# Gates, their picking rows and output biases as two rounded float32 parts instead of three bfloat16 ones

## The chip, the cores and the metric

The kernel runs on one core of a Trainium2 chip. The metric is the device time of one execution in microseconds. A run of the kernel before took 4008.13 us in the median of three (4006.91 to 4010.70).

## The reference, cut to what matters

The program is four blocks over x, an array of 2 x 1024 tokens by 128 features. Four of its parts are networks of experts, and they share one procedure in the kernel:

```
b0m: probs = softmax(flat @ Wr + br); only the top expert of 4 kept      (up 128->512, silu, down 512->128, + bias)
b0f: probs = softmax(xn @ router); top 4 of 16 kept, and 2 shared        (128->64, gelu, 64->128, no biases)
b1f: probs = softmax(xn @ gate); each of 8 experts takes its 256 best    (128->512, gelu, 512->128, + bias), and 1 shared
b3f: three trees (q, k, v) choose one of 16 leaves for each token        (128->64, relu, 64->128, + bias)
out[token] = sum over experts e of  gate[token, e] * (act(x @ W1[e] + b1[e]) @ W2[e] + b2[e])
```

Everything is float32 in the reference. The rest (a state space scan, attention of three kinds, six layers of local attention) is not touched by the change.

## The kernel before, in words

Tokens lie along the free dimension: x is a tile of 128 partitions (features) by 2048 columns (tokens), cut into 4 quarters of 512. TensorE takes three kinds of operands here: plain float32, bfloat16, and float32r, a rounded float32. A product of nearly float32 exactness is made from float32r parts: each operand is split into a head (the rounded value) and a tail (the rest), and three products are summed, head by head, tail by head, head by tail.

Each network stage is a chain of short stages with a barrier of all engines between them: `router_probs` (or `walk_trees` in b3f), `keep_top` (or `choose_tokens` in b1f), `to_part_rows` (`to_rows` in b3f), and `mlp`. Within a stage each engine runs its own list in order, and semaphores tie the lists together.

**Gates.** GpSimd first clears the tile `gates` (128 x 2048, bfloat16). `to_part_rows` splits the table of probabilities (tokens by experts) into three bfloat16 parts on VectorE (lines 1208 to 1215: copy, subtract, copy, subtract, copy), TensorE turns the 16 token tiles (line 346), and VectorE copies the turned parts from PSUM into the rows of `gates` (line 361). Before those copies VectorE also splits the output biases into three parts, with the same five instructions for each net. In b3f the gates are zeros and ones, so `to_rows` turns them whole, as plain float32 (line 313), but VectorE still splits three nets' biases before it copies (line 323).

**mlp.** A unit is (group g, quarter i, chunk c). There are 4 groups of 4 chunks in b0m, 9 of 1 in b0f, 9 of 4 in b1f and 24 of 1 in b3f, and with 4 quarters 64, 36, 144 and 96 units. For a unit TensorE issues:

- if the group is gated and c is 0, one bfloat16 product (line 449): a matrix `select` that picks and spreads the expert's gate rows, with `gates`. b0f and b1f have a last group without gates;
- three float32r products for the hidden layer (line 457);
- the output of the unit three places earlier: three float32r products (lines 474, 476, 479), preceded, where a net is opened, by three bfloat16 products of bias and gates (line 469).

ScalarE applies the activation function (line 519), VectorE multiplies by the gate (line 560), ScalarE rounds the product to its head (line 505) and VectorE subtracts for the tail (line 550). ScalarE (line 495) and VectorE (line 532) also split each group's weights, which SyncE's queue fetches (line 434).

Of the kernel before, what the change touches and what calls it, by code (L numbers as in the profile page):

```python
# [16 lines left out]
P = 128  # L17
B, T = 2, 1024
N = B * T
TILES = N // P  # L20
QW = 512
# [187 lines left out]
def router_probs(nc, K, name, flat, weight, bias_row, experts, probs, parts, gates, one_row=None):  # L209


    with ExitStack() as ctx:
# [6 lines left out]
        with stage(nc, "logits_ready", "shifted", "exps_ready", "headed", "tailed", "cleared",  # L219
                   "dve_chain") as (block, S):  # L220

            @block.gpsimd
            def _(pool):
                pool.memset(gates[:], 0.0).then_inc(S.cleared, 1)
                pool.wait_ge(S.cleared, 1)
                if one_row is not None:
                    pool.memset(gates[one_row:one_row + 1], 1.0).then_inc(S.cleared, 1)
                    pool.wait_ge(S.cleared, 2)
                take_tails(pool, flat, parts, S.headed, S.tailed)
# [64 lines left out]
def bias_parts(chain, dve, bias, parts, rest):  # L294

    for n in range(bias.shape[1]):
        split_parts(chain, dve, bias[:, n], [parts[:, n, i] for i in range(3)], rest[:])


def to_rows(nc, K, name, table, rows, short, bias, parts):  # L300


    with ExitStack() as ctx:
        M = Memory(nc, ctx)
        turned = M.ps(f"{name}_turned", [P, QUARTERS, QW])
        bias_rest = M.sb(f"{name}_bias_rest", [P, P])
        per = QW // P
        with stage(nc, "turned_ready", "copied", "dve_chain") as (block, S):
# [9 lines left out]
            @block.vector  # L318
            def _(dve):
                bias_parts(Chain(dve, S.dve_chain), dve, bias, parts, bias_rest)  # L320
                for q in range(QUARTERS):
                    dve.wait_ge(S.turned_ready, q + 1)
                    dve.tensor_copy(short[0:rows, cols(q, QW)], turned[0:rows, q]).then_inc(S.copied, 1)
                dve.wait_ge(S.copied, QUARTERS)

def to_part_rows(nc, K, name, table, rows, short, bias=None, parts=None):


    with ExitStack() as ctx:
        M = Memory(nc, ctx)
        turned = M.ps(f"{name}_turned", [P, QUARTERS, QW])
        split = M.sb(f"{name}_split", [P, TILES, 3, rows], BF16)
        rest = M.sb(f"{name}_rest", [P, TILES, rows])
        bias_rest = None if bias is None else M.sb(f"{name}_bias_rest", [P, P])
        per = QW // P
        wide = 3 * rows
        with stage(nc, "split", "turned_ready", "copied", "dve_chain") as (block, S):  # L340

            @block.tensor
            def _(pe):
                pe.wait_ge(S.split, 1)
                for t in range(TILES):
                    ins = pe.matmul(turned[0:wide, t // per, cols(t % per, P)],
                                    split[:, t].rearrange("p k e -> p (k e)"), K.ident16[:],
                                    start=True, stop=True)
                    if t % per == per - 1:
                        ins.then_inc(S.turned_ready, 1)  # L350

            @block.vector
            def _(dve):
                chain = Chain(dve, S.dve_chain)
                split_parts(chain, dve, table[:], [split[:, :, i] for i in range(3)], rest[:],
                            S.split)
                if bias is not None:
                    bias_parts(chain, dve, bias, parts, bias_rest)
                for q in range(QUARTERS):
                    dve.wait_ge(S.turned_ready, q + 1)  # L360
                    dve.tensor_copy(short[0:wide, cols(q, QW)], turned[0:wide, q]) \
                        .then_inc(S.copied, 1)
                dve.wait_ge(S.copied, QUARTERS)


# [2660 lines left out]
```

## Time and profile before

| | |
|---|---|
| median of three runs | 4008.13 us |
| profiled execution, its own time | 3999.94 us |
| its span, first to last instruction | 3998.2 us |
| TensorE busy | 3499.2 us (88%) |
| VectorE busy | 2983.8 us (75%) |
| ScalarE busy | 2425.5 us (61%) |
| the four mlp stages together | some 530 us of the span |

The span is that of one profiled execution, and 1.7 us of the execution lie around it. A busy matmul row includes the time in which a product drains under the next one, so the spacing of starts, and not the duration, tells what one product costs.

### The profile page before, as it was taken

How to read it: one execution, taken by the hardware profiler on the slowest of the kernel's cores; microseconds unless marked ns; L12 is line 12 of the kernel's file. 1: busy time of each engine (PE TensorE's matmuls, PEld its weight loads, DVE VectorE, ACT ScalarE, POOL GpSimd, SP SyncE). 2: the span in 40 equal slices, each digit the busy share in tenths (PEclk: the TensorE clock that was granted, in tenths of full speed). 3: DMA queues.
4: the chain of work that ended last, by engine and by line, in shares of the span. 5: the costliest groups of instructions: out<-in, count | busy, mean ns of one | idle time of the engine just before them, and what ended most of it. 6: DMA issues, size and time to landing. Idle time of an engine off the chain costs nothing. (4 is left out here: it accounts for less than half of the span.)

```text
span 3998.2 us, 103162 instructions
## 1 busy us (share of the span) xinstructions
PE 3499.2 (88%) x41084; PEld 2106.6 (53%) x41125; DVE 2983.8 (75%) x5780; ACT 2425.5 (61%) x4554; POOL 1393.6 (35%) x634
## 2 busy tenths in 40 slices
PE   7979678888849958999999999999999986998898
PEld 3347433333327735666666666666666663222665
DVE  5958757777739867777778777778778855887685
ACT  3336437777728826676666676676676652555472
POOL 3720011111100007676666675666666630000000
PEclk8979859999969979999999999999999996999899
DMA  1000047777602002322322322322322211100000
GB/s 40 0 6 6 11 161 231 232 232 231 196 12 69 11 0 64 98 61 56 99 60 59 97 59 58 99 57 62 97 58 63 58 42 59 35 25 13 14 15 11
DMA packets 174521, 285.75 MB, mean 71 GB/s; under 512 B 36819, under 2 KB 76628, under 8 KB 172116
## 3 DMA queue, kind: packets, MB, share of 16 engines
q1 hardware_dynamic: 173460, 278.40, 23.8%
q8 instruction: 329, 5.39, 0.6%
q14 instruction: 156, 1.28, 0.1%
q10 hardware_dynamic: 576, 0.69, 0.0%
HBM read 103.97 MB, written 74.45 MB: 45 GB/s over the span
## 5 line engine op out<-in xcount | busy, mean ns | idle before, releaser
L2298 POOL TENSOR_TENSOR b2f_norm<-b2f_norm,b2f_minus_half 128x16 f32<-128x16 f32 x192 | 555.1, 2909 | 275.5 <-DVE b2f_norm L2639 275.5
L2288 POOL TENSOR_TENSOR b2f_q<-b2f_q,b2f_q_part 128x1024 f32<-128x1024 f32 x96 | 228.1, 2376 | 693.7 <-DVE b2f_q_part L2629 693.7
L1720 ACT ACTIVATE b1a_weights<-b1a_b_ps 128x512 f32<-128x512 f32 x512 | 277.2, 596 | 39.4 <-PE b1a_b_ps L1645 37.2
L1835 DVE TENSOR_REDUCE b1a_tops<-b1a_a_ps 128x1 f32<-128x512 f32 (+3 forms) x512 | 244.6, 502 | 19.5 <-PE b1a_a_ps L1601 17.9
L2581 ACT ACTIVATE b2f_v_rows<-b2f_q_ps 128x1024 f32<-128x1024 f32 x96 | 98.3, 1024 | 262.6 <-PE b2f_q_ps L2360 153.5
L1552 POOL TENSOR_SCALAR b1a_k_op<-b1a_k_op,b1a_extra 128x1024 bf16<-128x1024 bf16 x32 | 90.7, 2845 | 446.5 <-DMA b1a_k_op<-part_copies 409.3
L1720 ACT ACTIVATE b3a_weights<-b3a_b_ps 128x512 f32<-128x512 f32 (+3 forms) x384 | 161.2, 502 | 136.8 <-PE b3a_b_ps L1655 135.6
L2638 DVE TENSOR_REDUCE b2f_norm<-xn 128x16 f32<-128x1024 f32 x192 | 234.2, 1220 | 12.0 <-ACT xn L2522 4.8
L2531 ACT ACTIVATE b2f_prob<-b2f_odd_ps,b2f_bias,b2f_norm 128x64 f32<-128x64 f32 x768 | 232.6, 447 | 6.2 <-DVE b2f_bias L2655 4.9
L2531 ACT ACTIVATE b2f_prob<-b2f_even_ps,b2f_bias,b2f_norm 128x64 f32<-128x64 f32 x768 | 232.6, 451 | 2.3 <-DVE b2f_bias L2655 2.3
L2291 POOL TENSOR_TENSOR b2f_k<-b2f_k,b2f_k_part 128x1024 f32<-128x1024 f32 x96 | 227.2, 2367 | 0.7 <-DVE b2f_k_part L2629 0.7
L1728 ACT ACTIVATE b1a_e_sb<-b1a_e_ps 128x512 f32<-128x512 f32 x256 | 153.0, 597 | 121.3 <-PE b1a_e_ps L1587 117.8
L2351 PE MATMUL b2f_q_ps<-b2f_wqkv,b2f_xs 128*128 128x512 f32 x384 | 212.2, 680 | 8.5 <-DVE b2f_kt L2605 5.7
L1830 DVE CUSTOM_DVE_ANT_0 b1a_summed<-b1a_a_ps,b1a_band 128x256 f32<-128x256 f32 (+2 forms) x320 | 142.4, 445 | 95.4 <-PE b1a_a_ps L1601 93.6
L2373 PE MATMUL b2f_q_ps<-b2f_o_cols,b2f_wo 128*128 128x128 f32 x1536 | 192.5, 279 | 4.2 <-ACT b2f_o_cols L2560 2.9
L2360 PE MATMUL b2f_q_ps<-b2f_wqkv,b2f_xs 128*128 128x512 f32 x384 | 190.6, 619 | 0.8 <-ACT xn L2522 0.8
L2351 PE MATMUL b2f_k_ps<-b2f_wqkv,b2f_xs 128*128 128x512 f32 x384 | 185.7, 606 | 0.0
L2373 PEld LDWEIGHTS b2f_q_ps<-b2f_o_cols,b2f_wo 128*128 128x128 f32 x1536 | 180.8, 193 | 6.4 <-ACT b2f_o_cols L2560 3.3
L712 POOL TENSOR_TENSOR b0s_drive<-b0s_raw,xn 128x1024 f32<-128x1024 f32 x32 | 135.1, 4222 | 89.9 <-DVE b0s_raw L728 89.9
L1601 PE MATMUL b1a_a_ps<-b1a_k_op,b1a_q_op 64*128 64x512 bf16 x512 | 139.5, 405 | 23.0 <-DVE b1a_tops L1835 22.5
L2625 DVE TENSOR_TENSOR b2f_q<-b2f_q_ps,b2f_turn 128x1024 f32<-128x1024 f32 x96 | 117.3, 1222 | 48.4 <-PE b2f_q_ps L2351 40.8
L2560 ACT ACTIVATE b2f_o_cols<-b2f_even_ps 128x1024 f32<-128x1024 f32 x48 | 49.2, 1026 | 149.8 <-PE b2f_even_ps L2366 149.7
(528 smaller groups left out, 9301.7 us busy)
## 6 DMA issues: line engine op xcount, KB each, us to landing
b2f_values<-b2f_v_rows SPq DMA_DIRECT2D x1534, 64.0 KB
position_scratch<-b1a_e_sb SPq DMA_DIRECT2D x128, 512.0 KB, 4.0
b1a_band<-position_scratch SPq DMA_DIRECT2D x128, 384.0 KB
b2f_wqkv<-in_b2f_wqkv SPq DMA_DIRECT2D x6, 1536.0 KB, 7.3
b2f_turn<-in_c_rotary SPq DMA_DIRECT2D x6, 1024.0 KB, 8.6
b1f_raw<-in_b1f_both SPq DMA_DIRECT2D x9, 512.0 KB, 3.7
part_copies<-b1a_parts SPq DMA_DIRECT2D x12, 256.0 KB
b2f_wo<-in_b2f_wo SPq DMA_DIRECT2D x6, 512.0 KB, 9.8
```

The costliest lines, as they stand in the source:

```text
L1720: act.activation(weights[:, s % P_RING, c, lo:QW], b_room(s, c)[:, lo:QW], ACT.Exp).then_inc(S.exps_ready, 1)
L1728: act.activation(e_sb[:, a % RING, h], e_ps[:], ACT.Copy).then_inc(S.e_copied, 1)
L1830: ins = dve.tensor_tensor_reduce(summed[:, n % 4, 0:z1 - z0], src, band[:, a % BANDS, h, at0:at0 + z1 - z0], 1.0, LOWEST, ALU.add, ALU.max ...
L1835: ins = dve.tensor_reduce(out, src, AX_X, ALU.max)
L2288: pool.tensor_tensor(G.q[:, g % 2], G.q[:, g % 2], G.q_part[:], ALU.add) \
L2291: pool.tensor_tensor(G.k[:, g % 2], G.k[:, g % 2], G.k_part[:], ALU.add) \
L2298: pool.tensor_tensor(part, part, G.minus_half[:, 0:HEADS], ALU.pow) \
L2351: pe.matmul((Z.q, Z.k)[j // 2][:, j % 2], tile_input(g), G.wqkv[:, l % 2, cols(j, QW)], start=True, stop=True).then_inc(S.qk_ready, 1)
L2360: ins = pe.matmul(Z.q[:, h], tile_input(g), wv[:, :, h], start=True, stop=True)
L2373: ins = pe.matmul(Z.q[:, 0, 0:P], G.wo[:, layer(g) % 2, p], G.o_cols[:, p], start=(p == 0), stop=(p == PAIRS - 1))
L2531: act.activation(G.prob[:, i // 2, i % 2], ps[:, i % 2, cols(i // 2, HD2)], ACT.Exp, bias=G.bias[:, i:i + 1], scale=G.norm[:, g % 3, i:i + ...
L2638: chain(dve.tensor_reduce(norm[:, cols(i, HEADS)], G.squares[:, i], AX_X, ALU.add))
```

## The change

The tile `gates`, the picking matrices and the output biases become float32r. The probabilities are split into two parts, head and tail, not three, and so are the biases; the picking matrices are repeated for two parts. Turned tables are plain float32 transposes in all four stages. The picking matrices arrive in bfloat16 as before, and ScalarE copies them to float32r within `to_rows`. The biases are split on GpSimd, one copy and one subtraction for all nets. The bias product at the opening of a net is two products in place of three.

```diff
-                pool.memset(gates[:], 0.0).then_inc(S.cleared, 1)
+                pool.memset(gates[:].bitcast(F32), 0.0).then_inc(S.cleared, 1)
...
+def to_rows(nc, K, name, table, rows, gates, pick, rounded, bias=None, split=True):
...
+        parts = M.sb(f"{name}_parts", [P, TILES, 2, rows], F32R) if split else None
...
+        wide = 2 * rows if split else rows
...
+                if split:
+                    pe.wait_ge(S.split, 2)
                 for t in range(TILES):
-                    ins = pe.transpose(turned[0:rows, t // per, cols(t % per, P)], table[:, t],
-                                       K.ident[:])
+                    src = parts[:, t].rearrange("p k e -> p (k e)").bitcast(F32) if split else table[:, t]
+                    ins = pe.transpose(turned[0:wide, t // per, cols(t % per, P)], src, K.ident[:])
...
+            @block.scalar
+            def _(act):
+                act.activation(rounded.pick[:], pick, ACT.Copy).then_inc(S.picked, 1)
+                act.wait_ge(S.picked, 1)
+
+            if bias is not None:
+                @block.gpsimd
+                def _(pool):
+                    pool.tensor_copy(rounded.bias[:, :, 0], bias[:]).then_inc(S.bias_headed, 1)
+                    pool.wait_ge(S.bias_headed, 1)
+                    pool.tensor_tensor(rounded.bias[:, :, 1], bias[:], rounded.bias[:, :, 0].bitcast(F32),
+                                       ALU.subtract).then_inc(S.bias_tailed, 1)
+                    pool.wait_ge(S.bias_tailed, 1)
...
-                bias_parts(Chain(dve, S.dve_chain), dve, bias, parts, bias_rest)
+                if split:
+                    dve.tensor_copy(parts[:, :, 0], table[:]).then_inc(S.split, 1)
+                    dve.wait_ge(S.split, 1)
+                    dve.tensor_tensor(parts[:, :, 1], table[:], parts[:, :, 0].bitcast(F32),
+                                      ALU.subtract).then_inc(S.split, 1)
...
-                        for n in range(3):
+                        for n in range(2):
                             pe.matmul(y_ps[:, i], nets[net].bias[:, n], gates[:, tokens(i)],
                                       start=(n == 0), stop=False)
...
-        gates = M.sb("b0f_gates", [P, N], BF16)
+        gates = M.sb("b0f_gates", [P, N], F32R)
```

The last edit is made alike for b0m, b1f and b3f.

## Rows read from the trace of the kernel before

**Rows 1.** The page, busy time of each engine over the span.
```profile
PE 3499.2 (88%) x41084; PEld 2106.6 (53%) x41125; DVE 2983.8 (75%) x5780; ACT 2425.5 (61%) x4554; POOL 1393.6 (35%) x634
```

**Rows 2.** Windows of the four mlp stages: b0m, b0f, b1f, b3f.
```profile
core 0: us, PE busy (x) PEld busy (x) DVE busy (x) ACT busy (x) POOL busy (x), PEclk, DMA share, GB/s
277.00:374.00 97.00, 95.83 (x400) 73.92 (x408) 86.81 (x146) 82.61 (x145) 0.00 (x0) 0.97 0.04 12
433.00:491.50 58.50, 56.98 (x238) 40.86 (x242) 45.57 (x75) 43.60 (x81) 0.00 (x0) 0.96 0.05 14
1198.00:1407.00 209.00, 207.78 (x887) 163.61 (x904) 184.72 (x309) 183.28 (x325) 0.00 (x0) 0.99 0.12 39
3735.00:3900.00 165.00, 163.71 (x689) 112.90 (x702) 134.33 (x222) 122.83 (x215) 0.00 (x0) 0.98 0.06 18
```

**Rows 3.** Waits in b3f's mlp, 3740 to 3895 us, longest first.
```profile
ACT b3f_hidden L519 <- PE b3f_h_ps L457: 36.7, 72, 1.1
DVE b3f_scaled L560 <- ACT b3f_hidden L519: 26.5, 65, 1.0
```

**Rows 4.** Timeline of TensorE, hidden layer's second product: first and last of stretches.
```profile
1230.22 0.40 PE L457 MATMUL b1f_h_ps<-b1f_xn_head,b1f_w_tail 128*128 128x512 f32 x1
...
1378.94 0.40 PE L457 MATMUL b1f_h_ps<-b1f_xn_head,b1f_w_tail 128*128 128x512 f32 x1
...
1384.42 0.39 PE L457 MATMUL b1f_h_ps<-b1f_xn_head,b1f_w_tail 128*128 128x512 f32 x1
...
1404.82 0.39 PE L457 MATMUL b1f_h_ps<-b1f_xn_head,b1f_w_tail 128*128 128x512 f32 x1
...
3754.02 0.39 PE L457 MATMUL b3f_h_ps<-b3f_xn_head,b3f_w_tail 128*128 128x512 f32 x1
...
3795.97 0.39 PE L457 MATMUL b3f_h_ps<-b3f_xn_head,b3f_w_tail 128*128 128x512 f32 x1
...
3805.10 0.39 PE L457 MATMUL b3f_h_ps<-b3f_xn_head,b3f_w_tail 128*128 128x512 f32 x1
```

**Rows 5.** Groups by line and form, TensorE: products and weight loads of b3f.
```profile
L457 PE MATMUL b3f_h_ps<-b3f_xn_head,b3f_w_head 128*128 128x512 f32 x96 | 56.6, 590 | 5.0 <-DVE b3f_w_tail L532 5.0
...
L449 PE MATMUL b3f_g_ps<-b3f_gates,b3f_pick 128*128 128x512 bf16 x85 | 33.7, 397 | 0.0
...
L457 PEld LDWEIGHTS b3f_h_ps<-b3f_xn_head,b3f_w_tail 128*128 128x128 f32 x96 | 18.7, 195 | 2.6
...
L449 PEld LDWEIGHTS b3f_g_ps<-b3f_gates,b3f_pick 128*128 128x128 bf16 x96 | 9.3, 97 | 31.2 <-issue 30.1 <-DVE b3f_scaled L560 1.0
```

**Rows 6.** Timeline of TensorE, plain float32 products of 512 columns, two a row.
```profile
1442.78 1.02 PE L1101 MATMUL b2a_kvr_ps<-xn,b2a_w_now 128*128 128x512 f32 x2
1443.64 1.02 PE L1103 MATMUL b2a_kvr_ps<-xn,b2a_w_ahead 128*128 128x511 f32 x2
```

**Rows 7.** Timeline, b3f's turning of the gates up to the mlp's first instruction.
```profile
3727.52 0.23 DVE L1208 CAST b3f_bias<-b3f_b 128x128 bf16<-128x128 f32 x1 [0.94 <-PEq L42]
3727.53 3.62 PE L313 MATMUL b3f_trees_turned<-c_ident,b3f_reach 128*96 128x128 f32 x16 [5.79 <-PEq L42]
...
3731.84 2.48 DVE L323 CAST b3f_gates<-b3f_trees_turned 96x512 bf16<-96x512 f32 x4
3735.23 0.42 ACT L495 ACTIVATE b3f_w_head<-b3f_raw 128x256 fp32r<-128x256 f32 x1 [30.69 <-PEq L42]
```

**Rows 8.** Timeline, b1f's split and turning of the gates.
```profile
1191.93 0.23 DVE L1208 CAST b1f_split<-b1f_probs 128x128 bf16<-128x128 f32 x1 [0.98 <-PEq L42]
1192.19 0.29 DVE L1209 TENSOR_TENSOR b1f_rest<-b1f_probs,b1f_split 128x128 f32<-128x128 f32 x1
...
1193.39 1.88 PE L346 MATMUL b1f_turned<-c_ident,b1f_split 128*24 128x128 bf16 x16 [3.94 <-DVE b1f_split L1215]
...
1194.68 2.47 DVE L361 CAST b1f_gates<-b1f_turned 24x512 bf16<-24x512 f32 x4
```

**Rows 9.** Groups by line and form, GpSimd and ScalarE: nearest rows for added or widened work.
```profile
L2305 POOL COPY b2f_kt<-b2f_kt 128x256 f32<-128x256 f32 x84 | 53.4, 635 | 0.0
L108 POOL TENSOR_TENSOR b1f_xn_tail<-xn,b1f_xn_head 128x512 fp32r<-128x512 f32 x4 | 5.1, 1294 | 3.4 <-ACT b1f_xn_head L101 3.4
...
L1317 POOL MEMSET b3a_values<- 128x256 f32 x1 | 0.6, 556 | 42.4 <-POOLq L42 42.4
...
L1396 ACT ACTIVATE b3a_parts<-b3a_left 128x1024 bf16<-128x1024 f32 x12 | 12.7, 1057 | 26.8 <-DVE b3a_left L1369 17.6 <-DVE b3a_left L1374 8.3 <-DVE b3a_left L1379 0.6
```

More of the change, by code:

```diff
@@ L291, in _, with rounded_constants @@
                 dve.wait_ge(S.counted, experts + 2)
[L294 to L300, printed above, removed]
+def rounded_constants(I, name, pick, nets):
+    return Names(pick=None if pick is None else I.sb(f"{name}_pick32", list(pick.shape), F32R),
+                 bias=None if nets is None else I.sb(f"{name}_bias", [P, nets, 2, P], F32R))
+def to_rows(nc, K, name, table, rows, gates, pick, rounded, bias=None, split=True):
     with ExitStack() as ctx:
@@ L305, in to_rows @@
         turned = M.ps(f"{name}_turned", [P, QUARTERS, QW])
-        bias_rest = M.sb(f"{name}_bias_rest", [P, P])
+        parts = M.sb(f"{name}_parts", [P, TILES, 2, rows], F32R) if split else None
         per = QW // P
-        with stage(nc, "turned_ready", "copied", "dve_chain") as (block, S):
+        wide = 2 * rows if split else rows
+        with stage(nc, "split", "turned_ready", "copied", "picked", "bias_headed", "bias_tailed") \
+                as (block, S):
             @block.tensor
@@ L322, in _ @@
                     dve.wait_ge(S.turned_ready, q + 1)
[L323 to L362, printed above, removed]
@@ L363, in _ @@
+                    dve.tensor_copy(gates[0:wide, cols(q, QW)], turned[0:wide, q]).then_inc(S.copied, 1)
                 dve.wait_ge(S.copied, QUARTERS)
@@ L604, in block0_ffn @@
             keep_top(nc, "b0f", probs, ROUTED0, TOP0)
-            to_part_rows(nc, K, "b0f", probs, ROUTED0, gates)
-        groups = [Names(net=0, select=K.pick16[:, c], biases=None) for c in range(pairs)]
+            to_rows(nc, K, "b0f", probs, ROUTED0, gates, K.pick16[:], rounded)
+        groups = [Names(net=0, select=rounded.pick[:, c], biases=None) for c in range(pairs)]
         groups.append(Names(net=0, select=None, biases=None))
@@ L821, in block0_attn @@
             rw, rb = weights.router, weights.router_b
-            gates = I.sb("b0m_gates", [P, N], BF16)
-            bias = I.sb("b0m_bias", [P, 1, 3, P], BF16)
+            gates = I.sb("b0m_gates", [P, N], F32R)
+            rounded = rounded_constants(I, "b0m", K.pick4, 1)
             parts = two_parts(I, "b0m_flat", [P, N])
@@ L828, in block0_attn @@
                 keep_top(nc, "b0m", probs, 4, 1)
-                to_part_rows(nc, K, "b0m", probs, 4, gates, b2, bias)
-            groups = [Names(net=0, select=K.pick4[:, e],
+                to_rows(nc, K, "b0m", probs, 4, gates, K.pick4[:], rounded, b2)
+            groups = [Names(net=0, select=rounded.pick[:, e],
                             biases=[b1[:, 4 * e + c:4 * e + c + 1] for c in range(4)]) for e in range(4)]
             mlp(nc, K, "b0m", parts, weights.stock, groups, ACT.Silu,
-                [Names(dst=flat, add=True, bias=bias[:, 0])], gates)
+                [Names(dst=flat, add=True, bias=rounded.bias[:, 0])], gates)
         layer_norm(nc, K, "b0n", flat, x, gain=w.ln_w, offset=w.ln_b, add_to=x)
@@ L1015, in block1_ffn @@
         b2 = later("b1f_b2", [P, 1, P])
-        gates = M.sb("b1f_gates", [P, N], BF16)
-        bias = M.sb("b1f_bias", [P, 1, 3, P], BF16)
+        gates = M.sb("b1f_gates", [P, N], F32R)
+        rounded = rounded_constants(M, "b1f", K.pick8, 1)
         parts = two_parts(M, "b1f_xn", [P, N])
@@ L1023, in block1_ffn @@
             choose_tokens(nc, w, probs, later.pairs)
-            to_part_rows(nc, K, "b1f", probs, EXPERTS1, gates, b2, bias)
-        groups = [Names(net=0, select=K.pick8[:, e] if e < EXPERTS1 else None,
+            to_rows(nc, K, "b1f", probs, EXPERTS1, gates, K.pick8[:], rounded, b2)
+        groups = [Names(net=0, select=rounded.pick[:, e] if e < EXPERTS1 else None,
                         biases=[b1[:, per * e + c:per * e + c + 1] for c in range(per)])
@@ L1028, in block1_ffn @@
         mlp(nc, K, "b1f", parts, stock, groups, ACT.Gelu_apprx_tanh,
-            [Names(dst=x, add=True, bias=bias[:, 0])], gates, fetch=fetch)
+            [Names(dst=x, add=True, bias=rounded.bias[:, 0])], gates, fetch=fetch)
 K_CLAMP, K_EPS = 60.0, 1e-8
@@ L2043, in block3_ffn @@
             reach = I.sb("b3f_reach", [P, TILES, 3, TREE_ROWS])
-            gates = I.sb("b3f_gates", [P, N], BF16)
-            bias = I.sb("b3f_bias", [P, 3, 3, P], BF16)
+            gates = I.sb("b3f_gates", [P, N], F32R)
+            rounded = rounded_constants(I, "b3f", w.pick, 3)
             parts = two_parts(I, "b3f_xn", [P, N])
@@ L2048, in block3_ffn @@
             to_rows(nc, K, "b3f_trees", reach[:].rearrange("p t n e -> p t (n e)"), 3 * TREE_ROWS, gates,
-                    w.b2, bias)
-            groups = [Names(net=n, select=w.pick[:, n, c], biases=[w.b1[:, n, c:c + 1]])
+                    w.pick[:], rounded, w.b2, split=False)
+            groups = [Names(net=n, select=rounded.pick[:, n, c], biases=[w.b1[:, n, c:c + 1]])
                       for n in range(3) for c in range(halves)]
-            nets = [Names(dst=qkv[n], add=False, bias=bias[:, n]) for n in range(3)]
+            nets = [Names(dst=qkv[n], add=False, bias=rounded.bias[:, n]) for n in range(3)]
             mlp(nc, K, "b3f", parts, w.stock, groups, ACT.Relu, nets, gates)
```

15 lines of the change are left out of this document (8 added, 7 removed).

## The prediction

> **What bounds the kernel now.** I read the page first, and it says little: TensorE is busy 88% of the span [rows 1], but that is a mean over stages that the change does not touch. So I went to windows over the four mlp stages [rows 2]. They last some 530 us, TensorE is busy for 98 to 99% of three of them and 97% of b0f, and VectorE and ScalarE for 75 to 88%. The waits of b3f confirm it [rows 3]: ScalarE waits for the hidden product 72 times, 36.7 us in all, and VectorE then waits for ScalarE. TensorE's order sets the pace, and the others have slack. A product less, or a shorter one, shows in the time at once.
>
> What a product costs is read from the spacing of starts [rows 4]. In b1f's last group, which has no gates, 15 units of six float32r products take 1404.82 - 1384.42 = 20.40 us: 1.360 us a unit, 0.2267 us a product. A gated block of b1f (four units, 24 float32r products and one bfloat16) takes (1378.94 - 1230.22) / 26 = 5.720 us. The float32r part of it would be 5.440, so the lone bfloat16 product costs 0.280 us, more than a float32r one. In b3f 26 units of six and one take 3795.97 - 3754.02 = 41.95 us: 1.6135 us each, of which the gate product is 0.2535. The four units with bias products take (3805.10 - 3795.97) / 4 = 2.2825 us, so three bfloat16 products add 0.669 us, or 0.223 each.
>
> So a change of format has a price, but a small one. The hidden product behind the gate product stands in the trace with 590 ns, against the gate product's own 397 [rows 5]. Read as a stall that would be 0.19 us for each of 176 gates, 34 us in all. The spacing says otherwise: the long row begins almost together with the product ahead of it, and the two together cost 0.48 to 0.51 us where two float32r products cost 0.453. I go by the spacing.
>
> **The mlp stages.** With the gate product in float32r I give it the slot of its six neighbours, 0.2267 us.
> - b3f and b0f, a gated unit: 7 x 0.2267 = 1.5867 in place of 1.6135, 0.0268 us less. b3f has 84 such units without a bias, 2.25 us; b0f has 32, of which the first 4 run while the stage fills, so 28, 0.75 us.
> - b3f's 12 units with a bias: 9 x 0.2267 = 2.040 in place of 2.2825, 0.2425 less, 2.91 us.
> - b1f and b0m, a gated block: 25 x 0.2267 = 5.667 in place of 5.720, 0.053 less; 28 and 12 blocks without a bias, 2.1 us.
> - their 4 + 4 blocks with a bias: 0.053 plus 0.669 - 2 x 0.2267 = 0.216, together 0.27, 2.2 us.
>
> The sum is 10.2 us. Could the other engines hold it back? b1f's gated units with six products already run at the 1.36 us pace with all of VectorE's and ScalarE's work, and the b3f unit stays at 1.587, so neither becomes the bound.
>
> Lower bound of this part: the gate product keeps its 0.25 to 0.28 us and only the bias product and its slot go. The gates' share is 2.25 + 0.75 + 2.1, and 0.5 within the bias units, 5.6 us, so 4.6 us remain. Upper cost, in the other direction: plain float32 products of 512 columns stand 0.43 us apart [rows 6]. If the new products took that, 216 of them (176 gates, 40 biases) would cost 216 x 0.20 = 43 us more than in my sum. But operands of both sides are float32r, as in the six neighbours that take 0.2267, so I take the neighbours' value.
>
> Weight loads. A bfloat16 load takes 97 ns, a float32r one 195 [rows 5]. The Trainium skill, in "TensorE: Matmul & The Clock Gate", section "Weight-path perf modes — Fast Weight Load (FWL) and DoubleRow", says that the fast load of weights applies to 128 weights of a type other than FP32; the two rows agree with it, and it speaks against the change, which gives up the short load. By that rule 216 loads of 0.1 us more would add some 21 us if nothing hid them, and the sum of this change would be a loss. The rows show loads of 195 ns hidden under each product of a steady stream: six of them fit in 1.360 us. I cost the loads at nothing; the product ahead of each is the cover.
>
> **The turning stages.** In b3f the transposes end at 3731.15, but VectorE copies only from 3731.84 to 3734.32, because it has split three biases first [rows 7]. With the biases gone the copies follow the transposes quarter by quarter, and the last ends one copy (some 0.68 us) after them: 3731.8, 2.5 us earlier. GpSimd takes the biases, 384 elements a partition: by its rows of 635 ns for 256 copied and 1294 ns for 512 subtracted [rows 9] about 0.95 + 0.97 us, and twice that would still be covered. ScalarE copies 3072 elements of picks, three times the 1057 ns row [rows 9], 3.2 us. Both start beside the transposes and have 4.3 us before they would be late. If reading bfloat16 doubled ScalarE's time to 6.4 us, 2.1 of the 2.5 us would be given back; I take the cover as given.
>
> In b1f [rows 8] the five split instructions run from 1191.93 to 1193.39; a cast and a subtraction end near 1192.5. The transposes become plain float32, 3.62 us for 16 as in b3f in place of 1.88. They end near 1196.1, the last copy near 1196.8, against 1197.15 before: 0.35 us less. b0m is alike with a shorter split, 0.2 us less. b0f has no biases; there the shorter split and the slower transposes cancel, and I put it at nothing, within 0.5 us. Together 3.0 us less.
>
> The clearing of gates writes twice the bytes. If GpSimd goes by elements it costs what it did. If it goes as its slowest row, 556 ns for 256 float32 elements [rows 9], 2048 take 4.4 us in place of 1.8; in b1f there are two of them, 5.3 us more, of which 3.4 are covered by GpSimd's own wait ahead of the tails: at most 1.9 us lost, once. I take nothing.
>
> **Sum.** 10.2 + 3.0 = 13.2 us off the profiled execution: its span goes from 3998.2 to 3985, and its own time of 3999.94 to 3986.7. That execution lay 8.2 us under the median of the runs shown, so against the median: 4008.1 - 13.2 = 3995 us.
>
> **The rivals.**
> - The gate product keeps the bfloat16 price, because what costs is the pass through another accumulator and another operand tile and not the format. For it: I have no row of a gate product in float32r. Against it: hidden and output products also change accumulator every third product and keep 0.2267. The gain is 13.2 - 5.6 = 7.6 us, time 4000.5. Chance 0.10.
> - The clock takes it back. TensorE's granted clock over the four stages is 0.97, 0.96, 0.99 and 0.98 [rows 2], so it is at 1.2 GHz for 5.8 + 4.7 + 4.2 + 6.6 = 21 us of them, all of it at their starts, after a turning stage in which TensorE is hardly busy. A half clock for 21 us costs 10.5 us. The turning stages now have other lengths and up to twice the TensorE time, so each start meets the clock at another moment; some 5 us either way is possible. Against 13.2 us the bad end gives 4000. Chance 0.09.
> - Slower: the float32r loads are not hidden at the gate and bias products. Their place is behind the unit's last output product; the load of the bfloat16 pick began only with its own product ("issue", 30.1 us for 96 in rows 5), so a longer load may stand in the open there. Price 216 x 0.195 = 42 us against my sum, 4037. It decides from 13.2 / 216 = 0.06 us exposed for no gain, and 0.10 for slower by over 0.2%. Against it: the six neighbours hide theirs. Chance 0.05. The plain float32 pace, 43 us, would give 4038 and is within this chance.
>
> **How the numbers follow.** My forecast has the remaining 0.76. A change within 0.2%, 8 us, is about what a measurement of this kernel cannot tell from none. The forecast is faster by over that, unless the clock or the median's own spread eats 5 us of it. The clock rival and the kept price lie just at the line, mostly inside it. So: faster 0.78, same 0.17, slower 0.05. The likeliest case's own range is 3990 to 4001. The range for 8 in 10 is 3988 to 4003: its upper end takes in the gain of 7.6 us with some clock loss, its lower end a kinder clock.
>
> **What would show it.** In the profile after: b3f's gated units 1.587 us apart and its bias units 2.04; b1f's gated blocks 5.667; the hidden product behind the gate product near 390 ns; its weight load starting under the product ahead. b3f's mlp starting 2.5 us sooner after the turning's start; no instruction of the turning stages ending after VectorE's last copy. The prediction is wrong if gated units stand 1.61 us or more apart, if ScalarE's pick copy or GpSimd ends a turning stage, or if the starts of the mlp stages spend much more or less than 21 us at the low clock.

## The result, and the profile after

The changed kernel took 3993.18 us in the median of 12 runs (3982.52 to 4003.23), the kernel before 4008.11 us in 12 runs beside it. The ratio is 0.9965, with a 95% interval of 0.9954 to 0.9976. That is 14 us less, faster by more than 0.2%; the forecast was 13.2 us less, at 3995 us.

The page after, and the windows of the four mlp stages b0m, b0f, b1f, b3f (as [rows 2]):

```profile
span 3989.2 us, 103143 instructions
...
PE 3506.6 (88%) x41105; PEld 2146.2 (54%) x41105; DVE 2973.8 (75%) x5746; ACT 2431.2 (61%) x4558; POOL 1399.8 (35%) x640
```
```profile
276.90:373.00 96.10, 95.46 (x408) 77.10 (x408) 87.69 (x147) 82.55 (x145) 0.00 (x0) 0.98 0.04 12
432.20:491.20 59.00, 58.49 (x247) 47.00 (x248) 47.03 (x78) 44.26 (x82) 0.00 (x0) 0.97 0.05 14
1201.90:1410.50 208.60, 207.90 (x904) 170.12 (x904) 186.00 (x312) 183.57 (x325) 0.00 (x0) 0.99 0.12 39
3733.00:3895.00 162.00, 160.87 (x696) 131.34 (x696) 135.98 (x226) 123.51 (x216) 0.00 (x0) 0.99 0.06 18
```

TensorE still sets the pace. Its busy time went up on the page, by 7.4 us, while the kernel got faster. The plain float32 transposes of b0m, b0f and b1f are busy for 3.6 us each in place of 1.9, which is 5.1 us of it. And 41 products of the kernel before have a weight load but no record of their own (41125 and 41084 in [rows 1]), none after (41105 and 41105). The rows also overlap, 0.39 us long and 0.227 us apart, so busy time is no measure here, and spacing is. The timeline of TensorE, the hidden layer's second product, first and last of the same stretches as in [rows 4]:

```profile
1231.26 0.39 PE L438 MATMUL b1f_h_ps<-b1f_xn_head,b1f_w_tail 128*128 128x512 f32 x1
...
1378.59 0.39 PE L438 MATMUL b1f_h_ps<-b1f_xn_head,b1f_w_tail 128*128 128x512 f32 x1
...
3750.74 0.39 PE L438 MATMUL b3f_h_ps<-b3f_xn_head,b3f_w_tail 128*128 128x512 f32 x1
...
3791.99 0.39 PE L438 MATMUL b3f_h_ps<-b3f_xn_head,b3f_w_tail 128*128 128x512 f32 x1
...
3800.15 0.39 PE L438 MATMUL b3f_h_ps<-b3f_xn_head,b3f_w_tail 128*128 128x512 f32 x1
```

A gated block of b1f takes (1378.59 - 1231.26) / 26 = 5.6665 us, a gated unit of b3f 41.25 / 26 = 1.5865 us, a b3f unit with bias products 8.16 / 4 = 2.040 us. Forecast were 5.667, 1.5867 and 2.040. The groups of b3f, as in [rows 5]:

```profile
L430 PE MATMUL b3f_g_ps<-b3f_gates,b3f_pick 128*128 128x512 f32 x96 | 38.2, 398 | 1.8 <-PEq L42 1.7
L438 PE MATMUL b3f_h_ps<-b3f_xn_head,b3f_w_head 128*128 128x512 f32 x96 | 37.9, 394 | 0.4 <-DVE b3f_w_tail L513 0.4
```
```profile
L430 PEld LDWEIGHTS b3f_g_ps<-b3f_gates,b3f_pick 128*128 128x128 f32 x96 | 18.3, 190 | 6.7 <-issue 1.9 <-DVE b3f_scaled L541 1.1
```

The row of 590 ns is down to 394 ns, and TensorE is faster by 0.027 us a unit, not by 0.196. The load of the picks went from 97 to 190 ns, but the idle time before it from 31.2 to 6.7 us: it now starts under the product ahead. The turning of b3f's gates, as [rows 7]:

```profile
3728.26 0.50 POOL L330 CAST b3f_bias<-b3f_b 128x384 fp32r<-128x384 f32 x1 [18.68 <-SPq L40]
3728.27 2.76 ACT L324 ACTIVATE b3f_pick<-b3f_pick 128x3072 fp32r<-128x3072 bf16 x1 [23.30 <-PEq L42]
3728.29 3.31 PE L318 MATMUL b3f_trees_turned<-c_ident,b3f_reach 128*96 128x128 f32 x16 [5.79 <-PEq L42]
3728.85 1.00 POOL L332 TENSOR_TENSOR b3f_bias<-b3f_b,b3f_bias 128x384 fp32r<-128x384 f32 x1
...
3731.09 1.28 DVE L345 CAST b3f_gates<-b3f_trees_turned 96x512 fp32r<-96x512 f32 x2 [0.17 <-PE b3f_trees_turned L318]
3733.30 0.42 ACT L476 ACTIVATE b3f_w_head<-b3f_raw 128x256 fp32r<-128x256 f32 x1 [2.27 <-PEq L42]
```

GpSimd ends at 3729.85, ScalarE at 3731.03, VectorE last at 3732.37: the copies bind, as forecast. The clearing of gates, twice the bytes, takes the same 1.81 us, so nothing was the right price for it.

To compare whole stages I took two lengths from each trace: "turning" is from the first instruction of the split (in b3f the first transpose) to the mlp's first weight head, "mlp" from there to the start of VectorE's last addition or copy of the stage's output out of PSUM. The last column is a part that no edit here touches, the six layers of local attention (b2f), from the first product of queries to the last matmul of the last layer.

| kernel | turning b0m, b0f, b1f, b3f | mlp b0m, b0f, b1f, b3f | turning, mlp in all | b2f |
|---|---|---|---|---|
| before | 5.9, 6.0, 6.2, 7.7 | 98.6, 61.6, 211.1, 168.1 | 25.8, 539.4 | 1825.8 |
| changed | 5.8, 6.0, 6.3, 5.0 | 96.1, 60.5, 208.5, 162.7 | 23.1, 527.8 | 1820.8 |
| changed again (e0) | 5.9, 6.0, 6.0, 5.3 | 96.2, 60.4, 208.7, 162.4 | 23.2, 527.7 | 1822.9 |

The touched stages lost 11.6 + 2.7 = 14.3 us. The two profiled executions as wholes differ by only 9.0 us (3999.94 and 3990.96): b2f took 5.0 us less, and the other untouched parts together 10.3 more. One of them is the stretch from b1f's mlp to b2f, 83.4 us before and 87.5 in the change; its second and third nine microseconds had a granted clock of 0.81 and 1.00 before, and of 0.62 and 0.62 in the change. In e0, the same kernel again, it took 83.4 us at 0.81 and 1.00. So the untouched parts scatter by as much as the change is worth, and the evidence on the mechanism is in the touched stages.

### The profile page after: what moved, and what is told of

It reads as the page before. It is cut to its first block and busy times, and to the rows that moved or that the text cites. A ratio compares the mean times of both kernels' runs of the same rounds, so it can differ in the third digit from the quotient of the medians.

```text
span 3989.2 us, 103143 instructions
## 1 busy us (share of the span) xinstructions
PE 3506.6 (88%) x41105; PEld 2146.2 (54%) x41105; DVE 2973.8 (75%) x5746; ACT 2431.2 (61%) x4558; POOL 1399.8 (35%) x640
## 3 DMA queue, kind: packets, MB, share of 16 engines
q14 instruction: 156, 1.28, 0.1%
## 5 line engine op out<-in xcount | busy, mean ns | idle before, releaser
L1817 DVE TENSOR_REDUCE b1a_tops<-b1a_a_ps 128x1 f32<-128x512 f32 (+3 forms) x512 | 244.6, 502 | 20.3 <-PE b1a_a_ps L1583 18.8
L1812 DVE CUSTOM_DVE_ANT_0 b1a_summed<-b1a_a_ps,b1a_band 128x256 f32<-128x256 f32 (+2 forms) x320 | 142.4, 445 | 96.2 <-PE b1a_a_ps L1583 94.1
L1583 PE MATMUL b1a_a_ps<-b1a_k_op,b1a_q_op 64*128 64x512 bf16 x512 | 139.9, 406 | 23.1 <-DVE b1a_tops L1817 22.7
```

Source lines behind the costliest of these rows:

```text
L1812: ins = dve.tensor_tensor_reduce(summed[:, n % 4, 0:z1 - z0], src, band[:, a % BANDS, h, at0:at0 + z1 - z0], 1.0, LOWEST, ALU.add, ALU.max ...
L1817: ins = dve.tensor_reduce(out, src, AX_X, ALU.max)
```

## The experiments

Two theories stood against each other. **Slots**: TensorE's order is the bound, a gate product in the format of its neighbours costs 0.2267 us in place of 0.25 to 0.28, a bias product less saves its slot, and VectorE's copies start sooner in b3f. **Clock**: the stages' starts at half clock moved, and made or ate the gain. Each ratio is taken against runs of the kernel before made beside it.

**The change once more (e0).** No edit.

> The changed kernel once more, as the measure for the others of this group. The theory of slots expects 13 to 15 us less than the kernel before, with b3f's gated units 1.587 us apart, its units with a bias 2.04 us, and b1f's gated blocks 5.667 us, as in the first profile after. If instead the gain came from the clock, the time would move by several us from run to run and the spacings would not stay.

Measured: ratio 0.9972 (0.9960 to 0.9984), median 3991.51 us against 4001.11. The stage lengths repeat those of the first profile within 0.3 us each (table). The gain is there again, and sits in the same stages.

**The format alone undone (e1).** Gates, picks and biases are bfloat16, everything else is the changed kernel. The gates have two bfloat16 parts, so they are less precise than in either kernel.

```diff
-        gates = M.sb("b3f_gates", [P, N], F32R)
+        gates = M.sb("b3f_gates", [P, N], BF16)
...
-    return Names(pick=None if pick is None else I.sb(f"{name}_pick32", list(pick.shape), F32R),
-                 bias=None if nets is None else I.sb(f"{name}_bias", [P, nets, 2, P], F32R))
+    return Names(pick=None if pick is None else I.sb(f"{name}_pick32", list(pick.shape), BF16),
+                 bias=None if nets is None else I.sb(f"{name}_bias", [P, nets, 2, P], BF16))
```

> The changed kernel with only the format undone: gates, picking matrices and biases are bfloat16 again, still in two parts, turned and split as in the changed kernel (the gates lose precision by it). If the mix of formats costs what the spacing said, b3f's and b0f's gated units go back to 1.6135 us and b1f's blocks to 5.720 us, and the kernel takes 5 to 6 us more than the changed one. If the mix costs nothing, the spacings stay at 1.587 and 5.667 and the time stays. If the fewer bias products and the turning stage were all of the gain, this version equals the changed one; then about 7.5 us would have had to come from them alone.

Measured: ratio 0.9985 (0.9972 to 0.9997), between before and the change, and 0.0013 above e0, 5 us. The intervals of e1 and e0 overlap, so the whole time alone does not show this step; the stages do. The timeline of TensorE in e1:

```profile
1235.21 0.39 PE L438 MATMUL b1f_h_ps<-b1f_xn_head,b1f_w_tail 128*128 128x512 f32 x1
...
1383.76 0.39 PE L438 MATMUL b1f_h_ps<-b1f_xn_head,b1f_w_tail 128*128 128x512 f32 x1
...
3747.80 0.39 PE L438 MATMUL b3f_h_ps<-b3f_xn_head,b3f_w_tail 128*128 128x512 f32 x1
...
3789.75 0.39 PE L438 MATMUL b3f_h_ps<-b3f_xn_head,b3f_w_tail 128*128 128x512 f32 x1
...
3798.01 0.39 PE L438 MATMUL b3f_h_ps<-b3f_xn_head,b3f_w_tail 128*128 128x512 f32 x1
```

b1f's block is back at 148.55 / 26 = 5.7135 us, b3f's unit at 41.95 / 26 = 1.6135, just the value of before. The turning stages kept their length (5.8, 6.0, 6.2, 5.0), the mlps took 535.1 us. So the 11.6 us of the mlps split: before to e1, two bias products for three, 4.3 us; e1 to the change, the format, 7.3 us. The spacings account for 5.5 of the 7.3.

The rest is in the clock at the stages' starts. From windows of 1 us over the first 20 us of each mlp, the time at the lower level of the clock (granted 0.50) is:

| kernel | b0m | b0f | b1f | b3f | in all |
|---|---|---|---|---|---|
| before | 6.4 | 4.1 | 3.7 | 6.1 | 20.3 |
| changed | 3.4 | 3.4 | 3.4 | 3.4 | 13.6 |
| e1 | 6.6 | 6.7 | 3.6 | 3.4 | 20.3 |
| e2 | 6.5 | 3.5 | 6.6 | 4.1 | 20.7 |
| e7 | 0.0 | 0.0 | 0.0 | 0.0 | 0.0 |

Between e1 and the change b1f and b3f have the same low clock, and they differ by 1.5 and 2.3 us, about what the spacings give (1.5 and 2.6). In b0m and b0f e1 has 3.2 and 3.3 us more of low clock, and there it takes 1.8 and 1.7 us more where the spacings give some 0.8 each. So about 1 us in each of these two stages goes with the clock, and the 4.3 us of the bias products, between kernels with 20.3 us of low clock each, are free of it in sum. At the lower clock the formats hardly matter: the gate product and the hidden product behind it take 0.87 us before and 0.85 in the change. Why the clock rose sooner in the change was not tested.

**A third bias product (e2).** The output differs by a tail added twice.

```diff
-                        for n in range(2):
+                        for n in (0, 1, 1):
```

> The changed kernel with a third bias product where a net is opened, in float32r like the others; it adds the tail of the bias a second time, so the output differs by that. The theory of slots expects one slot more in each of the 20 opening units: b3f's go from 2.04 to 2.267 us, 4.5 us in all. The time of one run cannot show it; the spacing can. If products into the same accumulator with the same gates were cheaper than a slot, the unit would stay under 2.25.

Measured, in one run: b3f's unit with a bias 2.265 us (from 3805.09 to 3814.15, four units), the others 1.5869. That is 0.225 us more than in the change, so the slot holds for the bias product too. The mlps took 535.0 us, 7.2 more than in the change, where 20 slots are 4.5. The other 2.7 us are again in first units: b0m's first five hidden products stand 1.28, 1.28, 1.28 and 2.82 us apart in e2, and 1.28, 0.99, 1.07 and 2.04 in the change, of which 0.23 is the slot. These 2.7 us, too, go with the low clock of the table above: b0m and b1f have 3.1 and 3.2 us more of it in e2 than in the change, and are 1.1 us longer each than one slot in four units explains. So the starts of these stages differ from one program to the next with the steady pace untouched.

**Gates twice, in bfloat16 (e4, on the kernel before) and in float32r (e5, on the change).** The output is unchanged: the second product starts its sum anew.

```diff
+                        pe.matmul(g_ps[:, k % 2], groups[g].select, gates[:, tokens(i)], start=True,
+                                  stop=True)
                         pe.matmul(g_ps[:, k % 2], groups[g].select, gates[:, tokens(i)], start=True,
                                   stop=True).then_inc(S.g_ready, 1)
```

> The kernel before with each gate product issued twice, bfloat16 both times. It splits the price of the lone bfloat16 product (0.2535 us in b3f, 0.280 in b1f) into the product and the change of format. If the change of format is what costs, the second product has no such price and adds 0.21 to 0.22 us: b3f's unit goes from 1.6135 to 1.83, b1f's block from 5.720 to 5.94. If the price belongs to a bfloat16 product itself, the second adds as much as the first: 1.867 and 6.00.

> The changed kernel with each gate product issued twice, float32r both times. By the theory of slots it adds exactly 0.2267 us: b3f's unit 1.813, b1f's block 5.893. So two gate products in bfloat16 (1.83 and 5.94 by the first theory) would still cost more than two in float32r, by a difference that shrinks with each product in a row, and three to five in a row would be cheaper in bfloat16.

Timeline of TensorE in e4, then in e5, the same 26 blocks of b1f and 26 units of b3f:

```profile
1243.32 0.39 PE L459 MATMUL b1f_h_ps<-b1f_xn_head,b1f_w_tail 128*128 128x512 f32 x1
...
1397.24 0.39 PE L459 MATMUL b1f_h_ps<-b1f_xn_head,b1f_w_tail 128*128 128x512 f32 x1
...
3773.00 0.40 PE L459 MATMUL b3f_h_ps<-b3f_xn_head,b3f_w_tail 128*128 128x512 f32 x1
...
3820.84 0.40 PE L459 MATMUL b3f_h_ps<-b3f_xn_head,b3f_w_tail 128*128 128x512 f32 x1
```
```profile
1242.23 0.39 PE L440 MATMUL b1f_h_ps<-b1f_xn_head,b1f_w_tail 128*128 128x512 f32 x1
...
1395.46 0.39 PE L440 MATMUL b1f_h_ps<-b1f_xn_head,b1f_w_tail 128*128 128x512 f32 x1
...
3772.20 0.39 PE L440 MATMUL b3f_h_ps<-b3f_xn_head,b3f_w_tail 128*128 128x512 f32 x1
...
3819.35 0.39 PE L440 MATMUL b3f_h_ps<-b3f_xn_head,b3f_w_tail 128*128 128x512 f32 x1
```

e4 took 4036.99 us and e5 4032.23 in one run each. In e5 the block is 5.8935 and the unit 1.8135: exactly one slot more. In e4 they are 5.920 and 1.840. Over the float32r part (5.440 and 1.360) one bfloat16 product costs 0.280 in b1f and 0.2535 in b3f, two in a row cost 0.480 in both, and three in a row (the bias products of before) 0.65 to 0.67, against 0.227, 0.453 and 0.680. The theory that the change of format is what costs holds in b1f, where the second product adds 0.20. In b3f the second adds 0.2265, more than I expected; there only 6 float32r products stand between two switches, and 24 in b1f. In numbers: the price of mixing is at most 0.053 us for a change to bfloat16 and back, and with three bfloat16 products in a row nothing is left of it. In e1 the pair of bfloat16 bias products adds 2.065 - 1.6135 = 0.4515 us, less than two slots, so the count in a row is not all.

The trace of the kernel before shows where the price sits. These are the hidden layer's second products around one block of b1f; the gate product stands between the first two:

```profile
1302.98 0.39 PE L457 MATMUL b1f_h_ps<-b1f_xn_head,b1f_w_tail 128*128 128x512 f32 x1
1304.58 0.40 PE L457 MATMUL b1f_h_ps<-b1f_xn_head,b1f_w_tail 128*128 128x512 f32 x1
1305.97 0.39 PE L457 MATMUL b1f_h_ps<-b1f_xn_head,b1f_w_tail 128*128 128x512 f32 x1
1307.34 0.39 PE L457 MATMUL b1f_h_ps<-b1f_xn_head,b1f_w_tail 128*128 128x512 f32 x1
1308.70 0.39 PE L457 MATMUL b1f_h_ps<-b1f_xn_head,b1f_w_tail 128*128 128x512 f32 x1
```

Over the 26 blocks the four units take 1.5985, 1.390, 1.371 and 1.360 us in the mean; in the change they take 1.5865 and three times 1.360. Of the 0.053 us only 0.012 fall in the unit with the gate product. The other 0.041 fall in the two units behind it, which hold float32r products alone. So 0.280 us is what the product costs the stream and not its own slot, and in b3f the next gate product comes after six float32r products, before the slower ones have run out. Why the float32r products behind a bfloat16 one run slower stays open.

**Gates in plain float32 (e6).**

```diff
-                        pe.matmul(g_ps[:, k % 2], groups[g].select, gates[:, tokens(i)], start=True,
+                        pe.matmul(g_ps[:, k % 2], groups[g].select.bitcast(F32),
+                                  gates[:, tokens(i)].bitcast(F32), start=True,
```

> The changed kernel with the gate product read as plain float32, operands and tiles otherwise the same. It prices the case that the prediction set aside as an upper cost: plain float32 products of 512 columns stand 0.43 us apart elsewhere. b3f's unit goes from 1.587 to 1.79 if only the product is longer, 176 x 0.20 = 35 us in all and the kernel near 4026; to 1.81 or more if the change between plain float32 and float32r has a price of its own, as the change to bfloat16 has.

Measured, in one run: 4098.55 us against 4012.05 for before beside it; the mlps took 641.4 us, 113.6 more than in the change. My number was wrong by a factor of three. Timeline of TensorE and the groups of e6:

```profile
3800.91 1.02 PE L430 MATMUL b3f_g_ps<-b3f_gates,b3f_pick 128*128 128x512 f32 x2
3801.36 0.80 PE L439 MATMUL b3f_h_ps<-b3f_xn_head,b3f_w_head 128*128 128x512 f32 x1
3802.00 0.40 PE L439 MATMUL b3f_h_ps<-b3f_xn_head,b3f_w_tail 128*128 128x512 f32 x1
```
```profile
L430 PE MATMUL b3f_g_ps<-b3f_gates,b3f_pick 128*128 128x512 f32 x192 | 98.2, 592 | 1.7 <-PEq L42 1.7
```

There are 96 gate products in b3f and 192 records: a plain float32 product leaves two, 0.43 us apart, so it costs twice what I read from [rows 6]. b3f's unit is 2.2465 us (3802.00 to 3860.41, 26 units), the gate product 2.2465 - 1.360 = 0.887 us, 3.9 float32r slots. The Trainium skill, in "FP8 and Floating Point Precision", section "TensorE Precision Notes", says that true FP32 takes four passes through the array, and the measured 3.9 slots agree.

**The bias split moved alone (e3, on the kernel before).** The five instructions for each net go to GpSimd's own list.

```diff
-                bias_parts(Chain(dve, S.dve_chain), dve, bias, parts, bias_rest)
...
+            @block.gpsimd
+            def _(pool):
+                bias_parts(Chain(pool, S.pool_chain), pool, bias, parts, bias_rest)
```

> The kernel before with one part of the change alone: the output biases, still three bfloat16 parts, are split on GpSimd beside the transposes, no longer on VectorE ahead of the copies. The theory of slots expects 2.5 to 2.7 us less from the turning of b3f, 0.5 us or less from those of b1f and b0m, and unchanged spacings in the mlps: some 3 us less in all, which is under what the whole time can show but plain in the stage. If GpSimd's fifteen small instructions for three nets are slower than 4.3 us, b3f gains less or loses.

Measured: ratio 1.0001 (0.9990 to 1.0013). b3f's turning went from 7.7 to 7.1 us only, b1f's stayed at 6.2. Timeline of b3f's turning in e3, VectorE's last copy and GpSimd's last instruction:

```profile
3723.32 0.29 POOL L1214 CAST b3f_bias<-b3f_b 128x128 bf16<-128x128 f32 x1 [18.11 <-ACTq L40]
...
3727.01 0.69 DVE L326 CAST b3f_gates<-b3f_trees_turned 96x512 bf16<-96x512 f32 x1 [0.17 <-PE b3f_trees_turned L313]
...
3729.22 0.29 POOL L1219 CAST b3f_bias<-b3f_trees_bias_rest 128x128 bf16<-128x128 f32 x1
3730.39 0.42 ACT L501 ACTIVATE b3f_w_head<-b3f_raw 128x256 fp32r<-128x256 f32 x1 [29.79 <-PEq L42]
```

VectorE was done at 3727.7, but GpSimd's fifteen small instructions ran until 3729.5 and the barrier waited for them. My condition of 4.3 us decided: they took 6.2. So moving the split alone is worth 0.6 us of the 2.7 that the change gains in b3f; the rest comes with two wide instructions, for two parts and all nets at once, in place of the fifteen.

**The bias split on VectorE (e9, and timed as e11, on the change).**

```diff
-            if bias is not None:
-                @block.gpsimd
-                def _(pool):
...
+                if bias is not None:
+                    dve.tensor_copy(rounded.bias[:, :, 0], bias[:]).then_inc(S.bias_headed, 1)
+                    dve.wait_ge(S.bias_headed, 1)
+                    dve.tensor_tensor(rounded.bias[:, :, 1], bias[:], rounded.bias[:, :, 0].bitcast(F32),
+                                      ALU.subtract).then_inc(S.bias_tailed, 1)
```

> The changed kernel with its bias split, two instructions for all nets, on VectorE ahead of the copies and no longer on GpSimd. VectorE waits there for the transposes in any case, so by the theory of queues b3f's turning stage stays at 5.0 to 5.3 us: what the change gained there came from two wide instructions in place of fifteen, and not from the other engine. If it was the other engine, the stage goes up by 1 us or more. VectorE's cast and subtraction of the probabilities (0.35 and 0.57 us in b1f beside GpSimd) go back towards 0.23 and 0.29 if GpSimd at work is what slowed them.

Turning: 5.5, 6.0, 5.5, 5.2 us. b3f's length is that of the change, so it doesn't matter on which engine the two wide instructions run. In b1f VectorE's split of the probabilities, first in the change, then in e9:

```profile
1195.64 0.35 DVE L339 CAST b1f_parts<-b1f_probs 128x128 fp32r<-128x128 f32 x1 [0.95 <-PEq L42]
...
1196.02 0.57 DVE L341 TENSOR_TENSOR b1f_parts<-b1f_probs,b1f_parts 128x128 fp32r<-128x128 f32 x1
```
```profile
1190.47 0.23 DVE L330 CAST b1f_parts<-b1f_probs 128x128 fp32r<-128x128 f32 x1 [0.96 <-PEq L42]
1190.73 0.29 DVE L332 TENSOR_TENSOR b1f_parts<-b1f_probs,b1f_parts 128x128 fp32r<-128x128 f32 x1
```

Beside a working GpSimd the two take 0.35 and 0.57 us, without it 0.23 and 0.29. The 0.23 and 0.29 us return in e10 and e11, which have the split on VectorE too. The Trainium skill, in "SBUF — State Buffer", section "Who interferes with whom", says that VectorE and GpSimd share a pair of ports under an exclusive lock, and that a VectorE instruction with two inputs in SBUF contends with a GpSimd instruction that reads SBUF. The longer rows agree with a wait for it, though not every row is longer: in b0m the two subtractions start together at 271.42, VectorE's takes the 0.23 us that it takes without GpSimd, and GpSimd's takes 0.54.

The single run of e9 took 3972.04 us, 20 under the change. The same kernel was run ten times more:

> e9 once more, timed. Its one run took 3972 us, 20 us under the changed kernel, while its touched stages explain 1 us of it. If that run was chance, the median comes back to 3988 to 3992, a ratio of 0.996 to 0.997. If the untouched attention layers take less time in every run of this program, the ratio stays at 0.993 and the layers at 1813 us or less in the profile.

Ratio 0.9973 (0.9960 to 0.9985), turning 22.8 us in all (b1f 5.8), b2f 1822.5 us where e9 had 1812.7: the 3972 was chance.

**TensorE kept busy (e7, then shorter e8, then with e9's edit as e10, on the change).** Products that nobody reads; e7 has two of 512 columns at each place, e8 and e10 one of 256 and one of 128:

```diff
                         ins.then_inc(S.turned_ready, 1)
+                pe.matmul(warm[:, 0:256], K.mean[:], K.ones[:, 0:256], start=True, stop=True)
...
+                pe.matmul(y_ps[:, 3, 0:128], K.mean[:], K.ones[:, 0:128], start=True, stop=True)
                 for u in range(n_units + lag):
```

> The changed kernel with four products added per network stage whose results nobody reads: two of 512 columns in plain float32 behind the 16 transposes, two more at the head of the mlp, where TensorE waits for its first weights. The clock rival says that each mlp starts at half clock and that a busier TensorE ahead of it lifts the clock sooner: the granted clock over the four mlp stages rises from 0.98, 0.97, 0.99 and 0.99 towards 1.00, and up to 9 us are saved. If the added products only sit in the open, each stage starts up to 1 us later and 2 to 4 us are lost.

Windows of the four mlps in e7:

```profile
277.60:373.80 96.20, 95.52 (x412) 76.97 (x412) 87.74 (x148) 82.58 (x145) 0.00 (x0) 1.00 0.04 12
430.90:490.70 59.80, 59.00 (x252) 46.85 (x252) 47.62 (x79) 44.27 (x82) 0.00 (x0) 1.00 0.05 14
1202.40:1411.00 208.60, 207.96 (x908) 170.04 (x908) 185.93 (x312) 183.62 (x325) 0.00 (x0) 1.00 0.12 39
3726.10:3887.60 161.50, 160.63 (x700) 131.07 (x700) 135.94 (x226) 123.49 (x216) 0.00 (x0) 1.00 0.06 18
```

The granted clock is 1.00 in all four, as the rival said. Yet the mlps are as long as in the change (527.6 us), since the added products hold back the first real ones (in b1f the first hidden product starts 2.05 us after the first weight head, in the change 0.93), and the turnings are 5.5 us longer (28.6). Ratio 0.9982 (0.9972 to 0.9993). Half the rival is shown: the starts do run at half clock, and work ahead of them lifts it. In the mlps the clock gave back what the added work cost there; with the turning stages the touched stages are 5.3 us longer than in the change, and the ratio is 0.0010, 4 us, above e0's.

> The changed kernel with two short unread products per network stage in place of e7's four long ones: 256 columns in plain float32 behind the transposes, 128 at the head of the mlp. In e7 the granted clock was 1.00 in all four mlps, but the long products delayed the turning stage's end by about 1.4 us and the first hidden product by 1.1 us. If the clock stays up with the short ones, the four stages together (turning and mlp) get 3 to 5 us shorter than in the changed kernel, and the whole 0.1% faster; if the clock falls back before the first product, they are as long as in the changed kernel or 1 us longer.

> The edits of e8 and e9 together on the changed kernel: the bias split in two instructions on VectorE, and two short unread products per network stage. The stages that the edits touch should take 22.3 us of turning and 526.5 us of mlp, 2 us less than in the changed kernel. If the whole is also 8 us or more under the changed kernel's ratio of 0.9965 to 0.9972, that cannot come from these stages, and the place to look is the part that no edit touches (the six layers of local attention, 1806 to 1826 us in the profiles so far).

e8: ratio 0.9952 (0.9938 to 0.9967), turning 23.3, mlps 526.3 us. e10: 0.9963 (0.9950 to 0.9976), turning 23.0, mlps 526.7. The touched stages are 1.3 and 1.2 us shorter than the change's, not 2 to 5. e8 is the lowest ratio of those from several runs, but its touched stages explain 1.3 us of the 8 that it seems to gain on e0; its profiled execution was short in b2f, which it doesn't touch. The matmuls into one tile of b2f in the change and in e8 (duration min/median/max in ns, first and last start in us):

```profile
L2333 PE MATMUL b2f_k_ps<-b2f_wqkv,b2f_xs x384: 592/592/1061, 1501.5 to 3240.8; 128*128 128x512 f32 x192
...
L2424 PE MATMUL b2f_k_ps<-b2f_hidden,b2f_w x144: 592/592/668, 1692.3 to 3318.7; 128*128 128x512 f32 x144
```
```profile
L2336 PE MATMUL b2f_k_ps<-b2f_wqkv,b2f_xs x384: 592/592/1061, 1504.1 to 3229.8; 128*128 128x512 f32 x192
...
L2427 PE MATMUL b2f_k_ps<-b2f_hidden,b2f_w x144: 592/592/668, 1691.7 to 3306.7; 128*128 128x512 f32 x144
```

From the first to the last start of these rows it is 1817.2 us in the change and 1802.6 in e8, for the same instructions. Over all profiles of this study the part of the table's last column took 1806 to 1826 us (1806.1 in e8), and in e10, with e8's edits, 1824.3. So e8 is not shown to beat the change: its advantage doesn't repeat in e10. The length did not follow which edit was made (e9 and e11 are one kernel: 1812.7 and 1822.5), but it goes with the clock. Windows of 3 us over the part give, for the time at the lower clock, 61.5 us in e8, 71.0 in e9, 76.1 in e7, 81.1 in e0, 89.7 in e10, 91.4 in e11, 91.6 in the kernel before and 93.0 in the change, and the lengths rise with it from 1806 to 1826 us, though not strictly (1820.8 in the change). Why the lower clock is granted for such different times stays open; I ran nothing on it.

## Why the prediction was right

Point by point, by its own steps:

- **TensorE's order is the bound of the mlps.** Right: each edit of one slot moved the spacing by that slot (e2 0.225, e5 0.227), with ScalarE and VectorE following.
- **A float32r gate product costs a neighbour's slot.** Right to the last digit: 1.5865 and 5.6665 us against 1.5867 and 5.667. The rival of the kept price is refuted.
- **The row of 590 ns is no stall of 0.19 us.** Right. Whoever had read it as one would have forecast 34 us; the format was worth 7.3 us. But the prediction put the price at the gate product and the one behind it, 0.48 to 0.51 us for the two, and the trace has most of it in b1f in the float32r products of the next two units. The sum stayed right because it was taken over whole units and blocks.
- **Size of the mlps' gain.** 11.6 us for 10.2. The bias products gave 4.3 for 4.6. The format gave 7.3 for 5.6; its steady part is 5.5, and the further 1.8 us lie at the starts, which the sum had left out. They go with the clock: b0m and b0f, the two stages in which e1 has more low clock than the change, hold all of them. Two slips on which nothing hangs: the lower bound counted 0.5 us for the gates within the bias units where its own terms give 0.7 (12 x 0.027 + 8 x 0.053), and VectorE is busy for 89% of b0m's window in [rows 2], above the 88% given.
- **Weight loads cost nothing.** Right: the longer load is hidden, and the rival of the open load is refuted (no spacing shows it).
- **Turning.** 2.7 us for 3.0. b3f gave 2.7 for 2.5. b1f and b0m together gave nothing for 0.35 and 0.2: the split there was costed at VectorE's rows alone, and beside GpSimd its two instructions in b1f take 0.92 us in place of 0.52 (e9). GpSimd's work on the biases was 1.5 us, less than the 1.9 estimated.
- **The bound from plain float32.** Wrong: 43 us were given, 0.66 us for each of the 176 gate products alone is 116 us. The row was read as one product where it holds one of two records. The forecast didn't hang on it, since I had taken the neighbours' value, but the upper end of that step was too low.
- **The clock.** Here the prediction missed, in its own terms. It put the term at nothing and named as a sign of being wrong that the starts would spend much more or less than 21 us at the low clock. They spent 13.6 us, against 20.3 before. It was a rival for taking time back; in the touched stages it gave some 2 us. In the untouched stretch behind b1f it took 4.1 us in the profiled execution of the change, and nothing in that of e0.
- **The whole.** That the medians came out 14.9 us apart, and the ratio at 14, so near to 13.2, is partly luck: the same kernel in e0 gave a ratio worth 11 us and medians 9.6 us apart. What repeats is the 14.3 us in the touched stages. The scatter that the range had to hold comes for the most part from elsewhere, b2f above all.

## What to carry to other kernels

Cost a product by the spacing of starts over some twenty repeats of a steady loop; durations of single rows include waits and drains that overlap, and a row may be only one of several records of an instruction. A product in another format than its neighbours cost up to 0.05 us more than its slot here, most of it in the products behind it, although its own weight load was the shorter; it paid to make a lone product match, and for three in a row it made no difference. Before calling the rest of a gain an effect of the edit, compare the time at the lower clock in the same stages. When small preparatory work stands ahead of a barrier, merge it into wide instructions before moving it to another engine: fifteen small ones on GpSimd outlasted everything else, two wide ones fitted on either engine. On GpSimd they lengthened VectorE's split beside them.

## What the runs showed of the hardware that I had not expected

- A plain float32 product of 512 columns leaves two records 0.43 us apart and costs 0.887 us between float32r products, 3.9 times their 0.2267.
- Two bfloat16 products in a row cost 0.480 us and one alone 0.280, with 24 float32r products between. Of the 0.053 us above a slot, 0.041 fall in the two units of float32r products behind.
- VectorE's subtraction of 128 elements took 0.57 us beside GpSimd and 0.29 without.
- Without added products the starts of the four mlps held 13.4 (e5) to 20.7 us at the lower clock from one program to the next, and 3 us more of it went with about 1 us more in b0m, b0f and b1f. In b3f the kernel before and e3 have 6.1 and 3.4 us of it, and 168.1 and 168.0 us of length.
- The untouched attention layers took 1806 to 1826 us in the profiles, more than the whole effect of the change, and the longer profiles have more time at the lower clock. A difference of 14 us in 4008 can be measured only over many runs, and must be found again in the stages that the edit touches.
